# Building a graph's count matrix on one core: the one-hot blocks of source positions made by GpSimd instead of VectorE

## The reference, cut to what matters

```python
x, src, dst = ...                       # (3125, 256), (53125,), (53125,)
agg = segment_sum(x[src], dst, 3125)    # layer 0, and with src and dst exchanged
deg = segment_sum(ones, dst, 3125)      # layer 1
```

## Time and profile before

| what | value |
|---|---|
| device time, median of 3 runs | 2877.63 us (2872.69 to 2881.21) |
| the profiled execution: its own time | 2889.01 us |
| the profiled execution: its span | 2886.9 us |
| TensorE busy | 2124.0 us, 74% |
| VectorE busy | 1501.7 us, 52% |
| ScalarE busy | 768.4 us, 27% |
| GpSimd busy | 341.2 us, 12% |
| the stage of the windows | about 153 to 474 us from the span's start |

### The profile page before, as it was taken

The page is one execution under the profiler, slowest core; times in us unless marked ns, Lnnn a source line. Parts: engine busy times, 40 slices in busy tenths (PEclk is TensorE's granted clock), DMA queues, the critical chain, the costliest instruction groups (busy, mean ns, idle before and its releaser), DMA issues. The chain is left out here.

```text
span 2886.9 us, 44422 instructions
## 1 busy us (share of the span) xinstructions
PE 2124.0 (74%) x12655; PEld 1717.0 (59%) x12655; DVE 1501.7 (52%) x4181; ACT 768.4 (27%) x1572; POOL 341.2 (12%) x383
## 2 busy tenths in 40 slices
PE   7678886553595235887659789954999975899893
PEld 4356664442443135777636567744888865899793
DVE  4499995776603975000166612246999845111113
ACT  4345553220100020222224100004666630111110
POOL 0000001001100100343200000000000000233231
PEclk9899998775586555999879899986999965999996
DMA  2023333000091011334330043203222011622835
GB/s 57 10 82 125 123 115 114 0 0 8 0 229 49 0 40 49 117 120 133 93 71 0 6 112 96 65 13 94 54 60 59 22 45 66 222 89 89 262 104 148
DMA packets 112421, 226.81 MB, mean 79 GB/s; under 512 B 15726, under 2 KB 69728, under 8 KB 112233
## 3 DMA queue, kind: packets, MB, share of 16 engines
q1 hardware_dynamic: 97376, 190.92, 22.8%
q0 software_dynamic: 11712, 32.00, 3.5%
q10 hardware_dynamic: 3270, 3.20, 0.3%
HBM read 161.40 MB, written 64.67 MB: 78 GB/s over the span
## 5 line engine op out<-in xcount | busy, mean ns | idle before, releaser
L1565 PE MATMUL experts_ps_h<-experts_xt,experts_w 128*128 128x128 f32 x1952 | 258.5, 289 | 60.0 <-DMA experts_b<-in_L_ffn_b 30.9
L1565 PEld LDWEIGHTS experts_ps_h<-experts_xt,experts_w 128*128 128x128 f32 x1952 | 249.8, 203 | 79.7 <-DMA experts_w<-in_L_ffn_w 34.4
L2161 PE MATMUL gat_ps_o<-Y,gat_prob_t 125*125 125x256 f32 x1250 | 274.2, 379 | 0.0
L2161 PEld LDWEIGHTS gat_ps_o<-Y,gat_prob_t 125*125 125x125 f32 x1250 | 233.0, 188 | 33.8
L827 PE MATMUL adj_ps_w<-adj_one_k,adj_one_s 128*125 128x500 bf16 x1000 | 178.1, 304 | 81.5 <-DVE adj_one_k L758 58.1
L1575 PE MATMUL experts_ps_o<-experts_w,experts_hid 128*128 128x256 f32 x976 | 231.8, 381 | 0.0
L1851 PE MATMUL gcn_ps_a<-Yp,gcn_adj 125*125 125x512 bf16 x625 | 205.9, 382 | 19.8 <-DVE gcn_acc L1867 9.9
L1638 DVE TENSOR_TENSOR experts_hid<-experts_gate,experts_ps_g 128x512 f32<-128x512 f32 x65 | 44.7, 688 | 328.0 <-ACT experts_gate L1615 328.0
L1602 ACT ACTIVATE experts_xt<-experts_ps_t 128x256 f32<-128x256 f32 x122 | 46.9, 384 | 625.2 <-PE experts_ps_t L1552 568.0
L1575 PEld LDWEIGHTS experts_ps_o<-experts_w,experts_hid 128*128 128x128 f32 x976 | 176.8, 191 | 19.2
L827 PEld LDWEIGHTS adj_ps_w<-adj_one_k,adj_one_s 128*125 128x125 bf16 x1000 | 98.2, 138 | 131.5 <-DVE adj_one_k L758 59.1
(11 more groups left out here) (356 smaller groups left out, 3828.5 us busy)
## 6 DMA issues: line engine op xcount, KB each, us to landing
experts_w<-in_L_ffn_w SPq DMA_DIRECT2D x84, 512.0 KB
adjacency<-adj_tile SPq DMA_DIRECT2D x25, 683.6 KB
adjacency_t<-adj_tile_t SPq DMA_DIRECT2D x25, 683.6 KB
up_adj_t<-adjacency_t SPq DMA_DIRECT2D x25, 683.6 KB
gcn_adj<-adjacency SPq DMA_DIRECT2D x25, 683.6 KB
gat_cnt<-adjacency_t SPq DMA_DIRECT2D x25, 683.6 KB
experts_w<-in_L_ffn_W SPq DMA_DIRECT2D x32, 512.0 KB
combine_got<-pair SPq DMA_DIRECT2D x20, 560.0 KB
```

The lines of the kernel that those rows point to most:

```text
L1565: last = nc.tensor.matmul(ps[b][:, h * 128:(h + 1) * 128], w[b][:, k, h * 128:(h + 1) * 128], xt[b][:, k, :], start=(k == 0), stop=(k == K ...
L2161: last = nc.tensor.matmul(ps_o[b][0:ROWS, 0:C], prob_t[:, s * ROWS:(s + 1) * ROWS], K.Y[:, s, :], start=(s == 0), stop=(s == TILES - 1))
```

## The change

The one-hot blocks of the four fixed chunks are no longer made by VectorE (L753 is gone). GpSimd makes them in a new routine `lows`: it loads `first` into a register itself, waits for `win_done` of window w-2, copies the four columns of `low_all` to a buffer at a fixed place (`low_here`, 128 x 4), waits for that copy, and makes four is_equal comparisons of 128 x 125, one for each chunk. TensorE gets a new wait before the first matmul of each window (`low_ready`). `sums` moves inside: it now runs for tile t-2 after window 1 of tile t, and no longer waits for `parts_free`. `more_s`, `more_k`, `key_here` and `one_k` stay with VectorE. No DMA is added or moved.

```diff
-        turned, turn_used = m.sem("turned"), m.sem("turn_used")
+        low_here = [m.sb(f"low_here{i}", (CH, FIXED)) for i in range(2)]
+        low_moved, low_ready, turned, turn_used = (m.sem(n) for n in ("low_moved", "low_ready", "turned", "turn_used"))
...
-            def sums(t, b, i):
+            def sums(t, b):
                 pool.wait_ge(parts_ready, t + 1 + START)
-                pool.wait_ge(parts_free, t + 2)
                 nc.gpsimd.tensor_tensor(two_parts[b][:], parts[b][:, 0:64], parts[b][:, 64:128],
                                         ALU.add).then_inc(half_summed, 1)
                 pool.wait_ge(half_summed, t + 1 + START)
-                nc.gpsimd.tensor_tensor(K.AGG[:, t, :], two_parts[b][:], parts[b][:, 128:192], ALU.add)
+                nc.gpsimd.tensor_tensor(K.AGG[:, bass.ds(t, 1), :].rearrange("p t f -> p (t f)"), two_parts[b][:],
+                                        parts[b][:, 128:192], ALU.add)
                 nc.gpsimd.tensor_copy(K.DEG[:, bass.ds(t, 1)], parts[b][:, 192:193]).then_inc(parts_free, 1)
-            two_by_two(pool, TILES, sums)
+
+            def lows(t, b, w):
+                win, half = t * WPT + w, (b * WPT + w) % 2
+                first = pool.value_load(table[:, bass.ds(win, 1)], min_val=0, max_val=CHUNKS)
+                pool.wait_ge(win_done, win + 1 + START)
+                carry(pool, m)
+                nc.gpsimd.tensor_copy(low_here[half][:], low_all[:, bass.ds(first, FIXED)]).then_inc(low_moved, 1)
+                pool.wait_ge(low_moved, win + 1 + START)
+                carry(pool, m)
+                for j in range(FIXED):
+                    last = nc.gpsimd.tensor_scalar(one_s[half][:, j, :], K.number_row[:, 0:ROWS], low_here[half][:, j:j + 1],
+                                                   None, ALU.is_equal)
+                last.then_inc(low_ready, 1)
+
+            def tile(t, b):
+                for w in range(WPT):
+                    lows(t, b, w)
+                    if w == 1 and (not isinstance(t, int) or t >= 2):
+                        sums(t - 2, b)
+
+            pool.wait_ge(table_ready, 1 + START)
+            tile(0, 0)
+            tile(1, 1)
+            with pool.Fori(1, TILES // 2) as i:
+                tile(i * 2, 0)
+                tile(i * 2 + 1, 1)
+            tile(TILES - 1, 0)
+            sums(TILES - 2, 1)
+            sums(TILES - 1, 0)
...
                                     win_key[:, bass.ds(win, 1)], None, ALU.subtract).then_inc(keyed, 1)
-                    v.tensor_tensor(one_s[half][:], K.number_row[:, None, 0:ROWS].to_broadcast((CH, FIXED, ROWS)),
-                                    low_all[:, bass.ds(first, FIXED)][:, :, None].to_broadcast((CH, FIXED, ROWS)),
-                                    ALU.is_equal)
                     dve.wait_ge(keyed, win + 1 + START)
...
                 pe.wait_ge(win_read, (win if w == 0 else win - 1) + START)
+                pe.wait_ge(low_ready, win + 1 + START)
                 fixed(0, True, False)
```

## The result

The changed kernel takes 3003.8 us (median of 4 runs, 2994.64 to 3011.63) against 2878.56 before: ratio 1.0443, 95% interval 1.0417 to 1.0468, so 125 us slower. I had forecast 2868, between 2848 and 2912.

The account below looks back on a forecast made before the run. VectorE, busy 47.9 of 50 us, was taken as the bound at 12.82 us a tile; GpSimd's loop, 7.88 + 12c with c = 0.38, gives 12.44, 9.5 us less over 25 tiles: 2868 us, range 2848 to 2912.

Parts of the forecast that it names:

- break-even, c = 0.41: Price in us of one GpSimd comparison of 125 columns above which the change was to make the kernel slower.
- c = 0.38: Assumed us per GpSimd comparison of 125 columns, near the select's 0.26 with most of the contention added.
- the upper end, 0.60: Highest us per GpSimd comparison: 0.46 for an instruction reading two operands per column, 0.60 when contended by VectorE.
- the prediction's own sign of being wrong: Wrong if the comparison is under 0.33 or over 0.42 us, `one_k` passes 0.5, or TensorE waits more for `one_k` than GpSimd.
- Rival 3: GpSimd's comparison: reading a value per partition makes it dear, 2904 us at c = 0.50, 2934 at 0.60; chance 0.27.
- The loop 7.88 + 12c: Loop through GpSimd and TensorE: three `lows`, `sums`, windows 2 and 3 with `down`, two hand-overs; 12.44 us a tile.
- 0, and 3 us at most: Stage's start: cost of GpSimd's first `lows`, running beside VectorE's first window, counted as 0, 3 us at most.
- VectorE's tile of 11.6 to 12.5 us: VectorE's time a tile after losing L753: 11.6 us undisturbed, up to 12.5 with GpSimd's disturbance of `one_k`.
- Rival 4: VectorE and GpSimd lock each other out for whole instructions: each `one_k` loses 0.26 us, 2940 us; chance 0.05.
- The lost slack of the queue: VectorE's queue: without L753 as cover a slow load of `first` counts whole, 0.96 and 0.58 us a tile.
- The two hand-overs of 0.15 us: Passing work between engines, twice in the loop through GpSimd and TensorE: about 0.15 us each, 0.30 a tile.
- Rival 1: TensorE or VectorE's queue becomes the bound at 11.6 to 12.1 us a tile, 2848 to 2859 us; chance 0.20.

Follow-up runs that it names:

- e2: Changed kernel with GpSimd's four instructions adding the value per partition instead of comparing with it: 3009.19 us, one run.
- e5: Changed kernel with GpSimd's four comparisons covering 64 of 125 columns, the rest of `one_s` set to zero once before: 2953.08 us, one run.
- e1: Changed kernel with GpSimd's four comparisons using the constants 0 to 3 instead of a value per partition: 2970.96 us, one run.
- e9: Kernel before the change, with GpSimd also making two comparisons of 125 columns a window into a buffer nobody reads: ratio 1.0035.
- e7: Changed kernel with GpSimd making two of four blocks, VectorE the others in one instruction, and a tiny early GpSimd comparison: ratio 1.0008 to the kernel before.
- e8: Changed kernel with GpSimd making one of four blocks, VectorE three in one instruction, and a tiny early GpSimd comparison: ratio 0.9996 to the kernel before.

## Why the prediction was wrong

- **The change's frame held.** GpSimd became the bound, VectorE's busy share fell, and the prediction's break-even, c = 0.41, was the right question. At c = 0.38 the plain sequence below and the 7 us at the start would still have left it a little faster, so the direction came from c.
- **The step that failed is c = 0.38.** Measured: 0.575 us from start to start alone, and 0.666 in the mean. Even the upper end, 0.60, was too low, and the prediction's own sign of being wrong, a comparison over 0.42, came. I took the select by comparison as the nearest row, 0.26 us for 128 columns, because it compares too. But e2 shows that comparing isn't the point, and e5 that this instruction works at 2.56 ns a column. The right neighbour was the addition with two inputs, 2.2 ns a column, which I had used for the upper end only. That end's 0.46 alone lacked the rest of the columns' price (125 x 0.36 ns = 0.045 us) and the 0.074 for the value per partition; with both it is 0.58.
- **Rival 3 had the right direction, but neither the main cause nor the price.** Its cause was the value per partition, which is 0.074 of the 0.32 us missed against the select; without that value (e1) the kernel is still some 100 us slower than before. The 0.27 it got, and 2904 to 2934 us, followed from a c that ended at 0.60.
- **The loop 7.88 + 12c is not the bound at a large c.** GpSimd's plain sequence is 5 x (0.47 + 4c) + 1.32 = 3.67 + 20c, and passes the loop from c = 0.53 on. I never wrote it down, because at 0.38 it gives 11.3. At 0.666 it gives 17.0 us a tile, where the loop gives 15.9 and 17.4 was measured. Rival 3's prices at 0.60 should have been 15.7 instead of 15.1 us. In between (e1: c = 0.574, 16.4 us; e5: 0.515, 15.7 us) neither formula is enough: GpSimd waits for TensorE there, 41 and 52 us.
- **"0, and 3 us at most" at the start was 7.0.** The trace of before had a hint. GpSimd's queue has the same MODIFY_POOL_CONFIG right behind the reduction, at 146.4 us, ahead of the first `sums`; it cost nothing there, because `sums` had to wait for its input until 175.8. The change put work that TensorE needs at once into that gap.

```profile
L674 POOLq MODIFY_POOL_CONFIG  x24: 5/6/98, 146.4 to 447.1; - x24
```

- **VectorE's part held in size.** A comparison of GpSimd was to cost VectorE 0.07 us; `one_k`'s median rose from 377 to 398 ns, and e9 gives 0.06 a comparison on VectorE's own instructions, 0.04 on the stage. VectorE's tile of 11.6 to 12.5 us itself was not put to the test, since VectorE waited. Rival 4, the lock for the whole instruction, would have cost `one_k` 0.26; it didn't come. The lost slack of the queue is seen in e7, where it ate part of the gain.
- **The two hand-overs of 0.15 us** had no row behind them. The rows after show 0.13 us from the end of a window's comparisons to TensorE's start (306.80 to 306.93); the term is too small to matter.
- **The best case was too good.** Rival 1 (11.6 to 12.1 us a tile) took VectorE's saving nearly in full. e7, with half of the blocks moved, has GpSimd off the path and still takes 12.8: slower instructions and waits for the queue take back 27 of the 33 us saved.

## What to carry to other kernels

Before giving elementwise work to GpSimd, find the price per column of just that instruction form on it; a select or a copy in the trace doesn't tell it (0.84 ns a column for the copy against 2.56 here). Then write the helper's plain sequence, all its instructions in one turn of the loop, beside the loops through other engines: the helper that frees a 96% busy engine must itself fit into the turn. And if it only just fits, don't count the freed time in full, for both engines slow each other and the freed one's queue may be next.

## What the runs showed of the hardware that was not expected

- GpSimd's TENSOR_SCALAR with a value per partition: 0.19 us fixed, 0.074 for the value, 2.56 ns a column for is_equal. At 125 columns add takes 11 ns more, and 4-byte input takes the same.
- The cost of sharing is lopsided: beside a VectorE that hardly rests, GpSimd's comparison goes from 0.587 to 0.774 us in the median (e9), and to 1.009 where there is one a window (e8), while VectorE's `one_k` goes from 0.377 to 0.401 (e9).

```profile
L692 POOL TENSOR_SCALAR adj_one_s<-number_row,adj_low_here x125: 597/1009/1257, 156.5 to 467.4; 128x125 bf16<-128x125 f16 x125
```

- The load of `first` by GpSimd's queue takes what VectorE's takes, 0.29 us in the median and 1.33 at the most (e7).

```profile
L685 POOLq TENSOR_LOAD <-adj_table x125: 284/290/1328, 151.4 to 469.1; - x125
```
